# Graph attention layer on one core: attention vectors folded on TensorE, and low weight parts moved to other places in the start

## What is computed

```python
def _gat_heads(x, adj, W, a):            # W: [H,F,O], a: [H,2O]
    Wh = jnp.einsum('bnf,hfo->bhno', x, W)
    f1 = jnp.einsum('bhno,ho->bhn', Wh, a[:, :O])
    f2 = jnp.einsum('bhno,ho->bhn', Wh, a[:, O:])
    e = f1[:, :, :, None] + f2[:, :, None, :]
    e = jnp.where(e > 0, e, LEAKY_ALPHA * e)
    e = jnp.where(adj[None, None] > 0, e, NEG_INF)
    attn = jax.nn.softmax(e, axis=-1)
    return jnp.einsum('bhnm,bhmo->bhno', attn, Wh)
h = jax.nn.elu(_gat_heads(x, adj, W_heads, a_heads))   # 4 heads, F = O = 512
out = jax.nn.elu(_gat_heads(h, adj, W_out[None], a_out[None])[:, 0])
y = jnp.maximum(out @ w1 + b1, 0.0) @ w2 + b2 + out
y = (y - mu) / jnp.sqrt(var + LN_EPS) * ln_gamma + ln_beta
result = _layernorm(x + y)
```

## Time and profile before

| | |
|---|---|
| Time, median of 3 runs | 2199.12 us (2198.6 to 2199.14) |
| The profiled execution's own time | 2199.19 us |
| Its span | 2197.4 us |
| PE busy | 2121.6 us, 97% |
| DVE busy | 1595.2 us, 73% |
| ACT busy | 909.7 us, 41% |
| POOL busy | 970.8 us, 44% |
| DMA moved | 131.89 MB, mean 60 GB/s |
| first matmul | 46.34 us after the span's start |

### The profile page before, as it was taken

How to read it: one execution, slowest core, us unless ns; L and a number is a source line. 1 busy time by engine, 2 the same in 40 slices (tenths; PEclk the granted TensorE clock), 3 DMA queues, 4 the chain that set the end, 5 groups by cost and what they waited for, 6 DMA issues and landing times.

```text
span 2197.4 us, 43176 instructions
## 1 busy us (share of the span) xinstructions
PE 2121.6 (97%) x13952; PEld 1932.6 (88%) x13952; DVE 1595.2 (73%) x3228; ACT 909.7 (41%) x2122; POOL 970.8 (44%) x1019
## 2 busy tenths in 40 slices
PE   0799999999999999999999999999999999999997
PEld 0799999999999999999999999999999988999996
DVE  6776666666666666676667676666666669999998
ACT  2444444444444444444444444444444444444443
POOL 5443333333333333333333333333333337777776
PEclk9999999999999999999999999999999999999999
DMA  4301111111111111111111111111111133334342
GB/s 139 120 30 39 44 38 38 38 38 39 42 45 41 42 38 38 38 38 38 38 38 38 38 38 38 38 38 38 38 41 41 39 106 120 139 118 140 120 141 87
DMA packets 72279, 131.89 MB, mean 60 GB/s; under 512 B 8752, under 2 KB 8752, under 8 KB 72240
## 3 DMA queue, kind: packets, MB, share of 16 engines
q1 hardware_dynamic: 72240, 131.40, 17.8%
HBM read 97.81 MB, written 33.55 MB: 60 GB/s over the span
## 4 chain that ended last, share of the span: by engine, by line
PE 94%; DVE 2%; issue 2%; POOL 1%; DMA 0%; ACT 0%; POOLq 0%; SPq 0%; DVEq 0%; ACTq 0%
PE h_ps L403 11%; PE h_ps L405 11%; PE h_ps L404 11%; PE t_ps L419 11%; PE t_ps L418 11%; PE t_ps L417 11%; PE x_ps L350 3%; PE h_ps L499 2%; PE h_ps L501 2%; PE h_ps L500 2%; PE t_ps L515 2%; PE t_ps L514 2%; PE t_ps L513 2%; PE h_ps L387 1%; PE h_ps L388 1%
## 5 line engine op out<-in xcount | busy, mean ns | idle before, releaser
L1048 POOL TENSOR_TENSOR h_lo<-h_full,h_hi 128x256 fp32r<-128x256 f32 x512 | 397.7, 777 | 1062.0 <-ACT h_hi L644 1052.6
L403 PE MATMUL h_ps<-g_hi,wh_hi 128*128 128x256 f32 x2048 | 589.9, 288 | 0.7 <-DVE g_lo L791 0.4
L405 PE MATMUL h_ps<-g_hi,wh_lo 128*128 128x256 f32 x2048 | 578.6, 283 | 0.0
L404 PE MATMUL h_ps<-g_lo,wh_hi 128*128 128x256 f32 x2048 | 577.4, 282 | 0.0
L863 DVE TENSOR_SCALAR h_full<-h_full 128x256 f32<-128x256 f32 x512 | 279.2, 545 | 408.8 <-ACT h_full L615 408.6
L419 PE MATMUL t_ps<-wo_hi,h_lo 128*128 128x512 f32 x1024 | 403.8, 394 | 0.0
L418 PE MATMUL t_ps<-wo_lo,h_hi 128*128 128x512 f32 x1024 | 402.8, 393 | 0.0
L417 PE MATMUL t_ps<-wo_hi,h_hi 128*128 128x512 f32 x1024 | 401.9, 392 | 0.0
L403 PEld LDWEIGHTS h_ps<-g_hi,wh_hi 128*128 128x128 f32 x2048 | 386.5, 189 | 13.9 <-DVE g_lo L791 0.6
L404 PEld LDWEIGHTS h_ps<-g_lo,wh_hi 128*128 128x128 f32 x2048 | 385.8, 188 | 12.2
L405 PEld LDWEIGHTS h_ps<-g_hi,wh_lo 128*128 128x128 f32 x2048 | 385.9, 188 | 0.0
(11 more groups left out here) (117 smaller groups left out, 3832.1 us busy)
## 6 DMA issues: line engine op xcount, KB each, us to landing
x_dup<-in_x SPq DMA_DIRECT2D x256, 128.0 KB, 2.6
attn<-in_x_t SPq DMA_DIRECT2D x64, 256.0 KB, 2.8
mid<-o_buf SPq DMA_DIRECT2D x64, 256.0 KB, 2.1
o_in<-mid SPq DMA_DIRECT2D x32, 512.0 KB, 3.7
x_again<-in_x SPq DMA_DIRECT2D x32, 512.0 KB, 4.3
out<-res SPq DMA_DIRECT2D x64, 256.0 KB, 2.1
wh_raw<-in_w_heads SPq DMA_DIRECT2D x4, 1024.0 KB, 11.8
wo_raw<-in_w_out SPq DMA_DIRECT2D x2, 2048.0 KB, 12.1
```

Source lines behind the costliest of these rows:

```text
L403: mm(to, w_hi, g_hi[:, h, ft, :], start=ft == 0, stop=False)
L404: mm(to, w_hi, g_lo[:, h, ft, :], start=False, stop=False)
L405: last = mm(to, w_lo, g_hi[:, h, ft, :], start=False, stop=ft == FT - 1)
L1048: tt(h_lo[:, v % RING, :], h_full[:, v % 2, :], h_hi[:, v % RING, :].bitcast(F32), ALU.subtract).then_inc(h_lo_done, 1)
```

## The change

The host now also passes every head's weights transposed (`w_heads_t`, 4 MB), and `a_heads` as `a_cols`: 128 partitions, and for each head and each block of 128 outputs 8 columns, of which the two of that head hold the vectors and the others zero. SP loads `a_cols`, then the transposed weights into `wt_raw` (in the place of `wo_raw`) with both `x_t` blocks of chunk 0 behind the first head, then head 0's straight weights, all 4 `x` blocks at once into `x_first` (in the place of `g_hi`), the other heads, and after a wait for `folded` both halves of `w_out`.

TensorE makes the 8 rows of `u` transposed in 16 fp32 matmuls, with the 8 columns of `a_cols` as the stationary operand and 512 columns of `wt_raw` moving, all into one bank. VectorE copies the rows out, TensorE transposes them in four pieces, VectorE copies `u`. The 32 reductions are gone. ScalarE rounds head 0 and the four `x` blocks, and the heads 1 to 3 only after `attn_t_round(0, 1)`. VectorE takes the low parts of head 0, between `logits_out(0)` and `scores(0)`. GpSimd does `diagonal(0)`, the low parts of the four `x` blocks, and after `attn_done` the 12 low parts of heads 1 to 3. In chunk 0 the second transpose goes to the bank `x_ps[1]` and waits for nothing. What follows the start is as before.

```diff
+        u_rows_ps, u_ps = t_ps[0]
...
+        attn_t_bank = lambda c, p: x_ps[p] if first_of(c) else x_ps[0]
...
             def load_head(h):
-                sp.dma_start(a_all[:, 2 * h:2 * h + 2, :].rearrange("p k o -> p (k o)"),
-                             a_heads[h:h + 1, :].partition_broadcast(P)).then_inc(a_heads_in[h], 16)
                 sp.dma_start(wh_raw[:, h, :, :], w_heads[h].rearrange("(a p) o -> p a o", p=P))\
                     .then_inc(wh_in[h], 16)
 
+            sp.dma_start(a_cols[:, :, :, :].rearrange("p h a j -> p (h a j)"), a_heads).then_inc(a_cols_in, 16)
+            for h in range(NH):
+                sp.dma_start(wt_raw[:, h, :, :], w_heads_t[h].rearrange("(a p) f -> p a f", p=P))\
+                    .then_inc(wt_in[h], 16)
+                if h == 0:
+                    for p in range(CP):
+                        load_x_t(0, p)
             load_head(0)
-            load_x(0, 0)
-            load_head(1)
-            load_head(2)
-            for p in range(CP):
-                load_x_t(0, p)
-            load_head(3)
-            for b in range(1, CB):
-                load_x(0, b)
-            load_wo(0)
+            for half in range(2):
+                sp.dma_start(x_first[half * N:(half + 1) * N, :, :],
+                             x[0:CB * N, :].rearrange("(b n) f -> n b f", n=N)).then_inc(x_first_in, 16)
+            for h in range(1, NH):
+                load_head(h)
+            sp.wait_ge(folded, 1)
+            for k in range(2):
+                load_wo(k)
...
                 if p == 0:
                     pe.wait_ge(attn_done, c + 1)
-                else:
+                elif not first_of(c):
                     pe.wait_ge(attn_t_lo_done, c * CP + p)
+                to = attn_t_bank(c, p)
...
-                    if first and v % OT == 0:
-                        pe.wait_ge(wh_lo_done, FT * (v // OT + 1))
+                    if first and v == 0:
+                        pe.wait_ge(wh_lo_first, FT)
+                    elif first and v % OT == 0:
+                        pe.wait_ge(wh_lo_done, FT * (v // OT))
...
-            pe.wait_ge(u_done, 2 * HEAD_TILES)
+            pe.wait_ge(a_cols_in, 16)
+            for h in range(NH):
+                pe.wait_ge(wt_in[h], 16)
+                for ot in range(OT):
+                    last = mm(u_rows_ps[0:2 * NH, :], a_cols[:, h, ot, :], wt_raw[:, h, ot, :],
+                              start=h == 0 and ot == 0, stop=h == NH - 1 and ot == OT - 1)
+            last.then_inc(folded, 1)
             pe.wait_ge(const_done, 1)
+            pe.wait_ge(u_rows_done, 1)
+            for ft in range(FT):
+                last = transpose(u_ps[:, ft * 2 * NH:(ft + 1) * 2 * NH], u_rows[0:2 * NH, ft * P:(ft + 1) * P],
+                                 ident[0:2 * NH, 0:2 * NH])
+            last.then_inc(u_ps_done, 1)
+            pe.wait_ge(u_done, 1)
...
-            for h in range(NH):
+            def head_round(h):
                 act.wait_ge(wh_in[h], 16)
                 for ft in range(FT):
                     act.activation(wh_hi[:, h, ft, :], wh_raw[:, h, ft, :], copy).then_inc(wh_hi_done, 1)
-                x_round(0, h)
+
+            head_round(0)
+            act.wait_ge(x_first_in, 32)
+            for b in range(CB):
+                act.activation(x_split[:, b, :], x_first[:, b, :], copy).then_inc(x_hi_done, 1)
             exps(0)
             attn_t_round(0, 0)
             attn_t_round(0, 1)
+            for h in range(1, NH):
+                head_round(h)
...
-            for i in range(HEAD_TILES):
-
-                h, ft = i // FT, i % FT
-                dve.wait_ge(wh_in[h], 16)
-                dve.wait_ge(a_heads_in[h], 16)
-                for j in range(2):
-                    after(dve, u_done, 2 * i + j - 1)
-                    nc.vector.tensor_tensor_reduce(
-                        out=h_ps[j][:, :], in0=wh_raw[:, h, ft, :], in1=a_all[:, 2 * h + j, :], scale=1.0, scalar=0.0,
-                        op0=ALU.mult, op1=ALU.add, accum_out=u[:, ft, j * NH + h:j * NH + h + 1])\
-                        .then_inc(u_done, 1)
+            dve.wait_ge(folded, 1)
+            nc.vector.tensor_copy(u_rows[0:2 * NH, :], u_rows_ps[0:2 * NH, :]).then_inc(u_rows_done, 1)
+            dve.wait_ge(u_ps_done, 1)
+            nc.vector.tensor_copy(u[:, :, :].rearrange("p f k -> p (f k)"), u_ps[:, 0:FT * 2 * NH]).then_inc(u_done, 1)
             logits_out(0)
+            for ft in range(FT):
+                dve.wait_ge(wh_hi_done, ft + 1)
+                tt(wh_lo[:, 0, ft, :], wh_raw[:, 0, ft, :], wh_hi[:, 0, ft, :].bitcast(F32), ALU.subtract)\
+                    .then_inc(wh_lo_first, 1)
             scores(0)
...
-            for i in range(HEAD_TILES):
+            diagonal(0)
+            pool.wait_ge(diag_done, 2)
+            for b in range(CB):
+                pool.wait_ge(x_hi_done, b + 1)
+                rest = x_split[N:P, b, :]
+                tt(rest, x_first[N:P, b, :], rest.bitcast(F32), ALU.subtract).then_inc(x_lo_done, 1)
+            pool.wait_ge(x_lo_done, CB)
+            pool.wait_ge(attn_done, 1)
+            for i in range(FT, HEAD_TILES):
                 h, ft = i // FT, i % FT
                 pool.wait_ge(wh_hi_done, i + 1)
-                pool.wait_ge(u_done, 2 * (i + 1))
                 tt(wh_lo[:, h, ft, :], wh_raw[:, h, ft, :], wh_hi[:, h, ft, :].bitcast(F32), ALU.subtract)\
                     .then_inc(wh_lo_done, 1)
-                if i == HEAD_TILES - FT - 1:
-                    diagonal(0)
-                    pool.wait_ge(diag_done, 2)
-                if ft == FT - 1:
-                    pool.wait_ge(wh_lo_done, i + 1)
-                    x_rest(0, h)
             chunks(pool, iteration)
```

More of the change, by code:

```diff
@@ L20, with build @@
 import numpy as np
-def build(nc, x, x_t, adj, w_heads, a_heads, w_out, a_out, w1, b1, w2, b2, gamma, beta, mid, out):
+def build(nc, x, x_t, adj, w_heads, w_heads_t, a_heads, w_out, a_out, w1, b1, w2, b2, gamma, beta, mid, out):
     import concourse.bass as bass
@@ L65, in build @@
             pass
+        with nc.sbuf_tensor("below_wt", [P, NH, FT, O], F32), \
+                nc.sbuf_tensor("wt_raw", [P, NH, OT, F], F32) as wt_raw:
+            pass
         with ExitStack() as feed_forward:
@@ L107, in build @@
         attn = sb("attn", [P, CP, NH, 2, N])
+        with nc.sbuf_tensor("x_first", [P, CB, F], F32) as x_first, \
+                nc.sbuf_tensor("a_cols", [P, NH, OT, 2 * NH], F32) as a_cols, \
+                nc.sbuf_tensor("u_rows", [P, F], F32) as u_rows:
+            pass
         g_hi = sb("g_hi", [P, NH, FT, T], F32R)
@@ L151, in build @@
         g_banks = h_ps + x_ps
+        u_rows_ps, u_ps = t_ps[0]
         ot_ps, hid_ps, y_ps = x_ps[0], h_ps, t_ps[CHUNKS % 2]
         adj_in, a_row_in = sem("adj_in"), sem("a_row_in")
-        a_heads_in = [sem(f"a_heads_in{h}") for h in range(NH)]
+        a_cols_in, x_first_in = sem("a_cols_in"), sem("x_first_in")
+        wt_in = [sem(f"wt_in{h}") for h in range(NH)]
         wh_in = [sem(f"wh_in{h}") for h in range(NH)]
@@ L246, in load_x @@
             def load_x(c, b):
-                after(sp, x_lo_done, c * CB + b)
+                sp.wait_ge(x_lo_done, c * CB + b)
                 for half in range(2):
@@ L365, in transpose_attn @@
                     pe.wait_ge(attn_done, c + 1)
-                else:
+                elif not first_of(c):
                     pe.wait_ge(attn_t_lo_done, c * CP + p)
+                to = attn_t_bank(c, p)
                 for h in range(NH):
                     twice = attn[:, p, h, :, :].rearrange("p d n -> p (d n)")
-                    last = transpose(x_ps[0][:, h * P:(h + 1) * P], twice, ident[:, :])
+                    last = transpose(to[:, h * P:(h + 1) * P], twice, ident[:, :])
                 last.then_inc(attn_t_ps, 1)
@@ L571, in x_round @@
             def x_round(c, b):
-                act.wait_ge(x_in, (c * CB + b + 1) * 32)
+                act.wait_ge(x_in, (c * CB + b + 1 - CB) * 32)
                 if b == 0:
-                    after(act, g_ps, c * GQ)
+                    act.wait_ge(g_ps, c * GQ)
                 act.activation(x_split[:, b, :], x_dup[:, :], copy).then_inc(x_hi_done, 1)
@@ L1117, in _ @@
             ff_iteration(LAST, 1, CHUNKS // 2)
-_INS = ["x", "x_t", "adj", "w_heads", "a_heads", "w_out", "a_out", "w1", "b1", "w2", "b2", "gamma", "beta"]
+_INS = ["x", "x_t", "adj", "w_heads", "w_heads_t", "a_heads", "w_out", "a_out", "w1", "b1", "w2", "b2", "gamma", "beta"]
 def kernel(**inputs):
@@ L1132 @@
     x_t = x.reshape(-1, 128, features // 128, 128).transpose(0, 3, 2, 1).reshape(-1, features)
+    heads = a["a_heads"].shape[0]
+    a_parts = a["a_heads"].reshape(heads, 2, -1, 128)
+    a_cols = np.zeros((128, heads, a_parts.shape[2], 2, heads), a_parts.dtype)
+    for h in range(heads):
+        a_cols[:, h, :, :, h] = a_parts[h].transpose(2, 1, 0)
     arrays = {
```

(3 more changed lines are left out.)

10 lines of the change are left out of this document (4 added, 6 removed).

## The result

The changed kernel takes 2181.31 us (median of 4 runs, 2180.37 to 2182.15) against 2199.11 us before (4 runs, 2198.6 to 2199.14): a ratio of 0.9919, 95% interval 0.9904 to 0.9935. That is 17.8 us less where 15.5 were predicted. The profiled execution took 2181.38 us with a span of 2179.6.

What follows compares the result with a forecast made beforehand. A 68 us start set by other engines, then TensorE, bounds the kernel. Logits -20.1, head 0's low parts +2.4 and first tile +2.2 make -15.5 us: 2199.2 to 2183.7 us, range 2178 to 2199 (main case 2179 to 2190).

Steps and rivals of the forecast that it cites:

- The bound: Whole kernel: a 68 us start set by other engines, then TensorE, busy 97% of the span, is the bound.
- Landings and fold: Start: first weights land at 9.6 us, and TensorE's 32 fold instructions, not the DMA, end at 26.0 us.
- the 4.6 taken from the gather: Fold's clock: TensorE reaches its fast level after 4.6 us without a gap, as in the first gather before.
- cold fold: Rival in the fold: 8 stationary columns don't bring the fast level; 2197.6 us, no measurable change; chance 0.18.
- double price: Rival in the fold: fp32 instructions cost 1.76 us at the slow level; 2225.7 us, slower; chance 0.03.
- half price: Rival in the fold: one instruction costs 0.23 us, so the last landing sets its end; 2179.1 us; chance 0.09.
- Logits: Behind the fold: logits start at 27.9 us instead of 46.34 and end at 29.8 instead of 49.94, 20.1 gained.
- Softmax, the term mis-sized: Ahead of `scores`: head 0's low parts on VectorE alternate with GpSimd's diagonals on the shared port; +2.4 us, +0.5 to +3.
- First tile: From softmax to first tile: gather starts earlier, but 12 ScalarE roundings delay `g_round`; +2.2 us, from +1 to +6.
- GpSimd hidden: GpSimd's 12 subtractions: first `h_lo` at 20.5 us after `attn_done`, TensorE asks at 21.3, so hidden by 0.8 us.
- warm fold: Main case: TensorE reaches the fast level during the fold, at full fp32 price; 2183.7 us; chance 0.70.

Runs made afterwards that it cites:

- undo_fold: Changed kernel with only the fold undone: VectorE makes `u` in 32 reductions again, no transposed weights, new order and `x` blocks at once kept; 2187.46 us.
- fold_quarter: Changed kernel with only one of each head's four fold matmuls made, all weights still waited for, result different; 2177.25 us.
- one_bank: Changed kernel with chunk 0's second transpose back in the first one's bank, with its wait for VectorE; 2182.17 us.
- round_early: Changed kernel with ScalarE's 12 roundings of heads 1 to 3 moved ahead of the first softmax exponential; 2176.65 us.
- early_and_warm: `round_early` with 22 unread fp32r matmuls of 512 columns put on TensorE between `spread` and the first transpose; 2176.27 us.
- prewarm: Changed kernel with 55 unread fp32r matmuls of 128 columns on TensorE ahead of the fold; 2186.02 us.
- both_early: `round_early` with VectorE's four subtractions for head 0 also moved ahead of its wait for the fold; 2174.56 us.
- fold_twice: Changed kernel with the whole fold made a second time into the same rows, same result; 2194.17 us.

## Why the prediction was right, point by point

- **The bound.** Right as a place: 17.1 of the 17.8 us lie ahead of the first tile. The prediction names why `u` was late (1.75 us for a reduction that meets a subtraction, 0.70 for another), but it prices only their removal, and books 20 us under the fold. `undo_fold` shows that two thirds of the gain are there without it, with the contention ended and the `x` blocks at once. The sum holds for the whole change; it doesn't divide it.
- **Landings and fold.** First landing 8.66 (9.6 said), fold to 25.33 (26.0), instructions 0.85 and 0.43 us apart (0.88 and 0.44). Weight loads of the fold, slow and then fast:

```profile
12.88 0.14 PEld L555 LDWEIGHTS t_ps<-wt_raw,a_cols 128*8 128x8 f32 x1 [0.71 <-issue]
13.73 0.14 PEld L555 LDWEIGHTS t_ps<-wt_raw,a_cols 128*8 128x8 f32 x1 [0.72 <-issue]
14.44 0.09 PEld L555 LDWEIGHTS t_ps<-wt_raw,a_cols 128*8 128x8 f32 x1 [0.57 <-issue]
14.87 0.09 PEld L555 LDWEIGHTS t_ps<-wt_raw,a_cols 128*8 128x8 f32 x1 [0.34 <-issue]
```

  The level rose between 13.73 and 14.44, in the sixth microsecond of the fold (4.6 said). In the other runs with a whole fold it rose 2.5 to 6 us in, so the 4.6 taken from the gather was a fair middle and no more. The cold fold and the double price fell by this, and the half price too: 16 matmuls of two instructions of 0.43 are the full fp32 price. (The half price was also worked out with a last landing at 19.5; `fold_quarter` has it at 17.9.) The four passes that the Trainium skill (FP8 and Floating Point Precision, TensorE Precision Notes) gives for it agree.
- **Logits.** Start 26.86 (27.9) and end 29.52 (29.8): -20.4 us where -20.1 was said. Two misses nearly cancel here, which is luck: the start came 1.0 us early, mostly by the landing, and the burst took 2.63 us instead of 1.9, as the level fell inside it. Windows of the changed kernel:

```profile
27.00:30.00 3.00, 2.49 (x16) 2.39 (x16) 0.41 (x3) 1.36 (x3) 0.00 (x0) 0.66 1.05 387
30.00:33.00 3.00, 0.00 (x0) 0.00 (x0) 3.00 (x4) 0.00 (x0) 2.75 (x2) 0.50 1.05 387
```

- **Softmax, the term mis-sized.** +2.4 us was said (0.5 to 3), +0.8 measured: from `logits_out` to the transposes 13.79 us against 12.96. The mechanism held: diagonals of 1.36 and 1.49 us instead of 1.04, and one subtraction of 1.76. But the scores came 1.67 later, not 2.6, and behind them 0.84 was saved where 0.2 was put, as GpSimd's last `x` block ends at 39.75 and `normalise` has the port to itself: L805 took 0.69 us, and 1.36 before. Of the 2.3 us between -15.5 and -17.8 this term makes 1.6. The terms as measured, -20.4 + 0.8 + 2.5, give the -17.1 at the first exponential; the last 0.7 come behind it and stay open.
- **First tile.** 16.05 us after the transposes against 13.56: +2.5 for +2.2. Gather at 3.4 as said, `g_hi` at 8.7 (9.25), TensorE idle 2.9 us in between (3.5). Two experiments take the term apart: the second bank gives 1.4 us (`one_bank`) and the place of the roundings costs 4.1 (`round_early`).
- **GpSimd hidden.** The 12 subtractions took 14.95 us, the first `h_lo` started 18.2 us after the transposes and ended at 19.4 (20.5), and no wait of TensorE names it. `early_and_warm` shows how near it is: the microsecond won ahead of its end came back as a wait for VectorE, which GpSimd held.

The Trainium skill (TensorE: Matmul & The Clock Gate, "What's actually happening") has the gate open by how busy TensorE has been, and the forecast of a warm fold rested on rows that it fitted. The fold agrees. `prewarm` doesn't as it reads: TensorE was busy without a pause for 12 us, and the fold's instructions behind it still started 0.85 us apart. The measurement decides; what set those short matmuls apart wasn't separated.

## What to carry to other kernels

A change of several parts can be predicted well in sum and read wrongly in parts: undo the part with the name in the title before giving it the credit, and do the others alone too, since here the freed port gave nothing in an order in which the `x` blocks then came late. Where two engines share a port, the place of the less urgent one can be worth as much as the operation that is removed, and a wait that keeps it behind the late engine can be faster than none (2.2 us in the medians here). Work that stands between a result and its reader on an in-order queue belongs to an idle stretch ahead of it: the two moves of `both_early` gave 6.7 us for no instruction less.

## What the runs showed of the hardware that wasn't expected

- Behind 12 us of back-to-back fp32r matmuls of 128 columns TensorE's spacing was still the slow one. It became the fast one 2.5 to 6 us into the fold's fp32 matmuls with 8 stationary and 512 moving columns. In `early_and_warm` the fp32r fillers of 512 columns began at 32.20 at a granted clock of 0.50 and had 1.00 from 36 us on.
- In the profile of the changed kernel the level fell inside the logits' burst (8 moving columns, 16 instructions; 2.63 us). Of the ten profiles with a whole fold, the burst took 2.5 to 3.1 us in five and 1.95 in the other five, among them `fold_twice`, `round_early` and `prewarm`, where the clock fell only behind it. So the burst as such doesn't lose the level.
- An fp32r matmul of 128 columns took 0.218 us in `prewarm`, ahead of a fold that began at the slow level. One of 256 columns takes the same at the slow level (0.21 apart in the gather of `early_and_warm`), so the half width won nothing.
- The granted clock in the profile's windows reads 1.00 until its first fall, though the spacing ahead of it is the slow one (8.66 to 13.73 us above). At a start the level is read from the spacing.
- The place in the fold at which the level rises moves between executions: the fold took 15.4 to 16.8 us (15.2 in `prewarm`). With the burst behind it, the logits' end lay between 27.6 and 29.7 us in the eight profiles whose order on TensorE is the same up to there. Single profiles differ by up to 2 us for that alone.
